# Two gated cross-attention layers over a shared context: keys and values projected by f32 matmuls instead of three f16 ones, and the preparation of a batch laid out anew

## What is computed

```python
x = x + tanh(g_xattn[0]) * L0_xattn(layernorm(x), ctx)         # differential attention
x = x + tanh(g_ffn[0])   * L0_ffn(layernorm(x))                # 8 experts, top 2, and a shared one
x = x + tanh(g_xattn[1]) * L1_xattn(layernorm(x), ctx, mask)   # masked attention, 16 heads of 8
x = x + tanh(g_ffn[1])   * L1_ffn(layernorm(x))

def L0_xattn(q_in, kv):
    q, k, v = q_in @ Wq.T, kv @ Wk.T, kv @ Wv.T                # 32 query/key heads of 4, 16 value heads of 8
    a1, a2 = softmax(q1 k1 / 2) v, softmax(q2 k2 / 2) v
    return rmsnorm(a1 - lam * a2) * subln * (1 - lam_init) @ Wp.T + bp
```

## Time and profile before

| what | value |
|---|---|
| median of 3 runs | 2584.38 us |
| lowest and highest of them | 2583.19 and 3398.32 us |
| the profiled execution, its own time | 2582.84 us |
| its span on the core | 2581.0 us |
| mean granted clock of TensorE | 0.953 |
| first exponential of layer 0 | 140.6 us after the start |
| DMA: read and written in HBM | 141.39 MB and 76.48 MB |

### The profile page before, as it was taken

The page is one execution under the profiler, slowest core; times in us unless marked ns, Lnnn a source line. Parts: engine busy times, 40 slices in busy tenths (PEclk is TensorE's granted clock), DMA queues, the critical chain, the costliest instruction groups (busy, mean ns, idle before and its releaser), DMA issues. The chain is left out here.

```text
span 2581.0 us, 66889 instructions
## 1 busy us (share of the span) xinstructions
PE 2352.3 (91%) x28024; PEld 1277.8 (50%) x28024; DVE 1802.4 (70%) x3165; ACT 1466.8 (57%) x2101; POOL 770.1 (30%) x926
## 2 busy tenths in 40 slices
PE   3699999999999999999995976999999999999798
PEld 2244444444444444444444852555555555555576
DVE  2588888887887888888864554767667767676454
ACT  2156666666666666666673322665566666656422
POOL 4213323333333243233323442121212122221232
PEclk8589999999999999999997986999999999999799
DMA  3533434534534434444401106565566565653100
GB/s 93 109 66 78 96 95 80 101 90 77 110 77 90 105 77 95 98 80 99 97 2 48 32 29 124 109 117 112 114 116 120 110 123 115 127 107 65 50 1 14
DMA packets 152931, 222.40 MB, mean 86 GB/s; under 512 B 45156, under 2 KB 102116, under 8 KB 152132
## 3 DMA queue, kind: packets, MB, share of 16 engines
q1 hardware_dynamic: 152644, 218.29, 40.5%
HBM read 141.39 MB, written 76.48 MB: 84 GB/s over the span
## 5 line engine op out<-in xcount | busy, mean ns | idle before, releaser
L959 ACT ACTIVATE probs<-score_ps 125x896 f32<-125x896 f32 x1152 | 1012.5, 917 | 261.0 <-PE score_ps L863 260.3
L1021 DVE TENSOR_REDUCE max_part<-max_ps 112x1 f32<-112x500 f32 x1538 | 992.2, 670 | 238.9 <-PE max_ps L844 129.3
L879 PE MATMUL acc_ps<-probs,vext 125*32 125x224 f32 (+1 forms) x12288 | 676.4, 315 | 7.1 <-issue 6.2
L1021 DVE TENSOR_REDUCE max_part<-spare_ps 112x1 f32<-112x500 f32 x766 | 513.5, 670 | 118.0 <-PE max_ps L844 105.5
L844 PE MATMUL max_ps<-kstack,qstack 48*112 48x500 f16 x1538 | 518.1, 401 | 25.7 <-DVE max_part L1021 12.9
L879 PEld LDWEIGHTS acc_ps<-probs,vext 125*32 125x32 f32 x12288 | 257.7, 108 | 305.9 <-issue 281.1
L863 PE MATMUL score_ps<-qstack,kstack 50*125 50x224 f16 (+1 forms) x6144 | 386.9, 243 | 1.9 <-ACT probs L959 1.7
L863 PEld LDWEIGHTS score_ps<-qstack,kstack 50*125 50x125 f16 x6144 | 303.6, 134 | 111.4 <-issue 53.4
L844 PE MATMUL spare_ps<-kstack,qstack 48*112 48x500 f16 x766 | 307.0, 401 | 14.9 <-DVE max_part L1021 7.2
L844 PEld LDWEIGHTS max_ps<-kstack,qstack 48*112 48x112 f16 x1538 | 167.0, 128 | 197.6 <-DVE max_part L1021 132.3
L740 POOL TENSOR_TENSOR heads_out<-turned,rden 56x64 f32<-56x64 f32 x192 | 55.2, 288 | 695.6 <-DVE rden L1012 685.5
(11 more groups left out here) (185 smaller groups left out, 2537.3 us busy)
## 6 DMA issues: line engine op xcount, KB each, us to landing
kstack<-k_parts SPq DMA_DIRECT2D x384, 187.5 KB, 6.5
k_parts<-khl SPq DMA_DIRECT2D x128, 375.0 KB, 5.5
ctx_in<-in_ctx SPq DMA_DIRECT2D x32, 750.0 KB
context_parts<-ctxT SPq DMA_DIRECT2D x32, 750.0 KB, 4.8
ctxT<-context_parts SPq DMA_DIRECT2D x32, 750.0 KB, 6.1
qrows<-q_parts SPq DMA_DIRECT2D x384, 7.0 KB, 7.4
qstack<-max_rows SPq DMA_DIRECT2D x384, 0.9 KB
mask_in<-in_mask SPq DMA_DIRECT2D x64, 82.0 KB
```

What stands on the lines that cost most here:

```text
L879: last = nc.tensor.matmul(acc_ps[32 * j:32 * j + 32, TT * S * i:TT * S * (i + 1)].rearrange("p (s c) -> p s c", s=S), vext[n % SLOTS][:, t ...
L959: nc.scalar.activation(probs[t % 2][:, 896 * h:896 * h + 896].rearrange("k (b c) -> k b c", b=2), score_ps[(t * H + h) % 2][0:KT, :, 0:448 ...
L1021: nc.vector.reduce_max(max_part[0:PIECE, u, third:third + 1], room(user)[0:PIECE, 0:TK], AX.X).then_inc(s_red, 1)
```

## The change

- The turned context stays in f32. `ctxT` (two f16 halves), `ctx_in` and `w_parts` go; one buffer `ctx_f` with two slots takes their place. In layer 0 slot 1 is the loaded context and slot 0 the turned one; in layer 1 the two slots hold the contexts of alternate batches, each with its semaphore. The DRAM copy `context_parts` is f32, the same bytes.
- K is one f32 matmul of 500 columns, V is four f32 matmuls of 128 columns. The weights are the f32 ones; the key weight of layer 0 is copied in another order of columns (`wk_order`). Value weights are no longer multiplied by 64.
- T has no low half: ScalarE's copy is all.
- In layer 1 ScalarE copies the keys with their bias to `key_f`, and GpSimd splits them (`split_keys`), as in layer 0.
- The table `where` places the users anew, one a step on side 1, and M on side 0 as before.
- In layer 1 the load of context `n+4` is issued where that of `n+3` stood, and waits for the values of batch `n+2`.

```diff
-        ctx_in = sb("ctx_in", [KT, NKT, D])
-        ctxT = sb("ctxT", [128, 2, SK], F16)
-        w_parts = sb("w_parts", [128, 2, 2, 2, D], F16)
+        ctx_f = sb("ctx_f", [128, 2, NKT * D])
+        wk_order = sb("wk_order", [128, D])
...
-                    for w in range(2):
...
-                        link(nc.vector.tensor_scalar(weight, weight, QK_UP, None, ALU.mult))
...
-                        link(nc.vector.tensor_copy(high, weight))
-                        link(nc.vector.tensor_tensor(low, weight, high, ALU.subtract))
+                    link(nc.vector.tensor_scalar(small[f"WkT{i}"][:, :], small[f"WkT{i}"][:, :], QK_UP, None, ALU.mult))
+                link(nc.vector.tensor_copy(wk_order[:, :].rearrange("p (r h x) -> p r h x", r=2, h=2), halves_first(small["WkT0"][:, :])))
...
     if L is L0:
-        where = {("V", 0): (0, 1), ("F", 0): (1, 0), ("V", 1): (1, 1), ("F", 1): (2, 0), ("V", 2): (2, 1),
-                 ("T", 0): (3, 1), ("K", 0): (4, 1), ("T", 1): (5, 1), ("K", 1): (6, 1), ("M", 0): (7, 0), ("T", 2): (7, 1),
-                 ("K", 2): (8, 1), ("A", 0): (9, 1)}
+        where = {("V", 0): (0, 1), ("F", 0): (1, 1), ("F", 1): (2, 1), ("V", 1): (3, 1), ("T", 0): (4, 1), ("V", 2): (5, 1),
+                 ("K", 0): (6, 1), ("M", 0): (7, 0), ("T", 1): (7, 1), ("K", 1): (8, 1), ("T", 2): (9, 1), ("K", 2): (10, 1),
+                 ("A", 0): (11, 1)}
     else:
-        where = {("V", 0): (0, 1), ("F", 0): (1, 0), ("V", 1): (1, 1), ("F", 1): (2, 0), ("V", 2): (2, 1),
-                 ("M", 0): (7, 0), ("K", 0): (7, 1), ("K", 1): (8, 1), ("K", 2): (9, 1), ("A", 0): (10, 1)}
+        where = {("V", 0): (0, 1), ("F", 0): (1, 1), ("V", 1): (2, 1), ("F", 1): (3, 1), ("V", 2): (4, 1), ("K", 0): (5, 1),
+                 ("K", 1): (6, 1), ("M", 0): (7, 0), ("K", 2): (8, 1), ("A", 0): (10, 1)}
...
                 if L.masked:
-                    sp.wait_ge(s_v, NTHIRD * n)
+                    at_least(sp, s_v, NTHIRD * (n - 1))
...
                     if L.masked:
-                        next_context(n + 3)
+                        next_context(n + 4)
...
-                if L is L0 and n + 3 < B:
+                if n + 3 < B:
                     split_keys(n + 3)
...
-                    for k, (w, x) in enumerate(((0, 0), (1, 0), (0, 1))):
-                        last = nc.tensor.matmul(spare_ps[:, 0:TK], Wk[w], ctxT[:, x, TK * i:TK * i + TK], start=k == 0, stop=k == 2)
+                    nc.tensor.matmul(spare_ps[:, 0:TK], Wk[:, :], ctxT[n % len(ctxT)][:, TK * i:TK * i + TK],
+                                     start=True, stop=True).then_inc(s_ready, 1)
...
-                        for k, (x, w) in enumerate(((0, 0), (0, 1), (1, 0))):
-                            last = nc.tensor.matmul(spare_ps[0:KT, D * t:D * t + D], ctxT[:, x, c:c + KT], Wv[w],
-                                                    start=k == 0, stop=k == 2)
+                        last = nc.tensor.matmul(spare_ps[0:KT, D * t:D * t + D], ctxT[n % len(ctxT)][:, c:c + KT], Wv[:, :],
+                                                start=True, stop=True)
...
-                    nc.scalar.activation(ctxT[:, 0, TK * i:TK * i + TK], spare_ps[:, 0:TK], ACT.Copy).then_inc(s_ctxT, 1)
+                    nc.scalar.activation(ctxT[0][:, TK * i:TK * i + TK], spare_ps[:, 0:TK], ACT.Copy).then_inc(s_ctxT, 1)
...
+                    at_least(act, s_kl, NTHIRD * (n - 1) + i + 1)
+                    key = key_f[:, TK * i:TK * i + TK]
+                    if L.masked:
+                        nc.scalar.activation(key, spare_ps[:, 0:TK], ACT.Identity, bias=small["bk1"][:, :]).then_inc(s_kf, 1)
...
-                    nc.vector.tensor_tensor(ctxT[:, 1, k], spare_ps[:, 0:TK], ctxT[:, 0, k], ALU.subtract).then_inc(s_cl, 1)
...
-                    nc.vector.scalar_tensor_tensor(khl[:, 1, TK * i:TK * i + TK], spare_ps[:, 0:TK], small["bk1"][:, :],
-                                                   khl[:, 0, TK * i:TK * i + TK], ALU.add, ALU.subtract).then_inc(s_kl, 1)
```

More of the change, by code:

```diff
@@ L478, in attend @@
     qstack = [T["qstack"][i][:, 0:PAIRS * GC].rearrange("p (c q) -> p c q", c=PAIRS) for i in range(SLOTS)]
-    Wk, Wv = ([T["w_parts"][:, layer, w, part, :] for part in range(2)] for w in range(2))
+    Wk, Wv = (small["WkT1"] if L.masked else T["wk_order"]), small[f"WvT{layer}"]
     S = L.heads // VH
@@ L984, in drain @@
                 kind, n, i = user
-                if kind in "VAF" or (kind == "K" and L is L0):
+                if kind != "M":
                     return
```

83 lines of the change are left out of this document (29 added, 54 removed).

## The result

| what | before | after |
|---|---|---|
| median | 2585.3 us | 2607.85 us (2607.45 to 2610.76, 4 runs) |
| ratio | 1 | 1.0092, 95% interval [1.0073, 1.0112] |
| span of the profiled execution | 2581.0 us | 2606.4 us |
| first exponential of layer 0 | 140.6 us | 135.4 us |
| a batch of layer 0 between output copies | 39.34 us | 39.24 us |

The forecast was 2412 us in a range of 2390 to 2470. It was wrong, in sign too. By the 2% that the prediction allows for, the measured time counts as no change; the interval lies above 1 all the same. One of the four runs before stood alone at 3398.32 us, and the ratio leaves it out.

A forecast was written before the change was run, and what follows sets the result against it. It took a TensorE - VectorE - TensorE chain to bound layer 0 and TensorE layer 1. Savings of 94 + 65 (batches), 9 + 2 (prologues) and 2 (setup) made 172 off 2582.8; with 1.5 for the median, 2412 us, range 2390 to 2470.

The forecast's parts named there:

- the price of an f32 product: TensorE, both layers: 0.11 us per 128-column f32 matmul; four for values 0.55, one of 500 columns for keys 0.53.
- the keys' far bound: Key projection, both layers: 0.95 us for the 500-column f32 matmul if an f32 column cost as much as four f16 ones.
- Values and keys: TensorE projections, both layers: f32 instead of f16 matmuls save 0.87 us a batch on values and 0.60 on keys.
- The low half on VectorE: Layer 0: dropping VectorE's context subtraction frees the first reduction, 0.55 us for each of three, 1.65 a batch.
- the three-bank reading of layer 0: Layer 0: a TensorE - VectorE - TensorE chain sets the step; the fourth piece waits until the first is reduced; 2.44 us.
- F to side 1, spreading: Layer 0: moving F off the spot between the pairs saves 0.04 us each, 0.1 a batch; spreading itself worth little.
- Layer 1's keys to GpSimd: Layer 1: three 0.74 us subtractions leave VectorE, saving 0.34 of waits and 0.4 of backlog a batch; search hides GpSimd's work.
- Two buffers: Layer 1's context loads: no gain in steady state and none expected in the prologue, between 0 and 5 us.
- The prologues and the setup: Before the layers: 9 us from layer 0's prologue, 2 from layer 1's, 2.4 from fewer weight operations in setup.
- (a): Rival, values and keys: f32 columns cost four f16 ones, values 0.98, keys 0.95, total 2565 us; chance 0.05.
- (b): Rival, layer 1: batch stays 25.1 us through later context load and queued maxima rows, 2477 us; chance 0.12, whole or part.
- (c): Rival, layer 0: key rows arrive late for search at step 7, slower than before, e.g. 2615 us; chance 0.03.

The follow-up runs named there:

- e7: The kernel after, with each key product taking 250 of its 500 columns from the fourth batch on: 2538.5 us.
- e2: The kernel before with f16 products, the turned context's low half left out (zero) and layer 1's keys split by GpSimd: 2534.7 us.
- e1: The kernel after with the kernel before's table of places in both layers: 2615.5 us.
- e6: e5 with the old places in layer 1, keeping two context buffers and the later load: 2536.8 us.
- e9: e6 with layer 1's context load, query rows and mask all issued behind the maxima's rows: 2596.7 us.
- e13: e6 with layer 1's query rows, key fills and context loads left out after the first batches (mask load stays): 2504.1 us.
- e5: e4 with VectorE making the first three batches' low halves, and two context buffers and the new places in layer 1: 2529.0 us.
- e12: e6 with layer 1's query rows loaded behind the maxima's rows: 2534.8 us.
- e11: e5 with layer 1's query rows loaded behind the maxima's rows: 2520.7 us, ratio 0.9725.
- e4: The kernel before with f16 products, ScalarE copying the turned context as f32 and GpSimd splitting it and all keys; nothing left out: 2548.2 us.

## Why the prediction was wrong

**The step that failed** is the price of an f32 product. The prediction put it so: "four f32 matmuls of 128 columns take 0.55 until the next instruction, and in the feed-forward stage 32 in a row take 3.66 us, 0.11 each". Both rows were misread.

- The four of the earlier trace rows (L819) turn a block; they are transposes, recorded once each. A transpose takes about half the time of a product: four of 125 columns are 0.58 above, four products of 128 columns 1.07.
- The 32 of the earlier trace rows are sixteen products: by the code an expert's down projection has four token tiles of two products, eight an expert. So one is 3.66 / 16 = 0.23 us.
- A count would have shown it. In the earlier trace rows the weighing of half a step is four products in the code and x8 in the row.

"Both rows give the same rate" was taken for a confirmation; two wrong readings agreed, since each of the two records of a product is about as long as the one record of a transpose. Against it stood the Trainium skill, "FP8 and Floating Point Precision", section "TensorE Precision Notes", four passes for true FP32. The trace agrees with it: 1.68 ns a column in e7, and 0.23 us for 128 columns in the earlier trace rows, where four passes at 2.4 GHz make 0.213 (an estimate). I had given it one chance in twenty. The prediction did write down 0.95 as the keys' far bound, but left it out of the range, where it would have been 3 x 0.42 x 58 = 73 us.

**Values and keys.** Forecast -0.87 and -0.60 a batch, measured +0.69 and +0.90. That is 3.06 us a batch off in each layer; over the 29 batches of each that still prepare another, 177 of the 196 us that the forecast missed.

**The low half on VectorE.** 1.65 forecast, 1.62 measured (e2). The number bears out the three-bank reading of layer 0. All of it went into the f32 products: 39.34 - 1.62 + 1.59 - 0.07 = 39.24.

**F to side 1, spreading.** Layer 0: 0.1 forecast, 0.07 measured (e1, which moves all users and not F alone). Layer 1: nothing forecast; it costs 0.41 a batch and saves 16 us of extra in this kernel, 27 in the f16 one. This was not in the prediction, and neither was the DMA load behind it: the earlier trace rows with 6.2 us of waits on "issue" was set down as noise of 10 us, where a cause with up to 46 us stood behind it: TensorE's instructions coming late.

**Layer 1's keys to GpSimd.** 0.74 forecast, 0.78 measured. The cover held, no search waited for a fill. Layer 1 in sum: 25.12 + 1.59 - 0.78 + 0.41 = 26.34.

**Two buffers.** Nothing forecast for the batch, nothing found: the regular batch is 24.34 in e2 with one and in e6 with two. (With f16 products and one buffer TensorE waits 5.2 us in all for the context, in e2 between 1600 and 2340 us; with two, nothing.)

**The prologues and the setup.** Forecast 9 + 2.4 for layer 0, measured 5.2. The kernel before, then the kernel after, TensorE's timeline of the first turning and of the keys of two thirds:

```profile
40.45 0.62 PE L794 MATMUL spare_ps<-wide,ctx_in 125*128 125x125 f32 x4 [2.58 <-PEq L324]
...
92.85 1.41 PE L803 MATMUL score_ps<-ctxT,w_parts 128*128 128x500 f16 x3 [1.55 <-DVE ctxT L992]
```

```profile
38.30 0.62 PE L781 MATMUL spare_ps<-wide,ctx_f 125*128 125x125 f32 x4 [2.57 <-PEq L315]
...
83.63 2.00 PE L789 MATMUL score_ps<-ctx_f,wk_order 128*128 128x500 f32 x2 [0.77 <-ACT ctx_f L917]
...
87.24 2.00 PE L789 MATMUL score_ps<-ctx_f,wk_order 128*128 128x500 f32 x2 [0.77 <-ACT ctx_f L917]
```

The setup gave 2.15 of 2.4. The wait of keys for the turned context fell from 1.55 to 0.77, the 0.78 of the forecast. Yet the key products hold TensorE for 1.80 (83.63 to 85.43) instead of 1.19 (89.06 to 90.25), at a granted clock of 0.50 between 80 and 90 us, and a third now takes 3.61 instead of 3.79 (the earlier trace rows and the row above): 0.18 gained where 1.18 was reckoned. Nine thirds make 1.6, and the two waits for the next context fell from 15.2 to 14.3 us in all. From layer 0's last exponential to layer 1's first 0.6 came of the 2 forecast for layer 1's prologue; the dearer keys are the likely reason, which no run separates.

**The rivals.** (a) was the right cause and had 2565 us. It priced the values at 0.98 and the keys at 0.95 by the rate of f16 columns; measured were 1.07 and 1.04. That is 0.09 x 6 = 0.54 a batch in each layer too little, 31 us over 58 batches, and it knew nothing of the 0.41 in layer 1, another 12: with the two it is 2608. That this meets the measured time so closely is luck: it leaves out the 7 us by which layer 1's extra fell, and some 3 that prologues and end gave less than (a) had. (b) did not come: no batch waits for a context or a maxima row. (c) did not come in the kernel after either (TensorE waits for no DMA between 140 and 1200 us), but e9 shows in layer 1 that the mechanism is real.

## What to carry to other kernels

Before a row prices an operation, divide its count by the number of operations that the code issues there, and ask whether it is a product or a transpose: an f32 product stands as two matmul records, a transpose as one. Three f16 products of high and low halves cost less here than one f32 product, and the gain of the idea lay in taking the splitting off VectorE: with f16 products kept and GpSimd splitting, the kernel runs at 0.9725 [0.9687, 0.9763] of the time before. When TensorE stops in the middle of a run of matmuls with no semaphore to wait for, look at the DMA share of that stretch and at when its instruction packets land, not at the engines.

## What the runs showed of the hardware that was not expected

- An f32 product of 500 columns takes 1.04 us until the next instruction, 250 columns 0.62, four of 128 columns 1.07; f32 transposes of 125 columns take 0.58 for four.
- TensorE stalls for up to 2.9 us inside uninterrupted matmuls while the DMA engines are full (e6), 22.1 us in 740; with most transfers gone there are none (e13). After the stall of 2.84 us the granted clock was 0.81 over 8.8 us.
- These stalls end 1.2 to 1.9 us after a 16 KB instruction packet has landed (all 110 in thirteen traces), and stand at one place of every block of 256 of TensorE's matmuls and weight loads.
- The same transfers and the same engine work went with 36 us or 9 us of irregular time, by where in the batch the preparation lies (e6, e5; 30 and 9 in e12 and e11).
- On GpSimd a cast of 128x500 from f32 to f16 takes 0.60 us and the subtraction 1.07: harmless a batch ahead, 14 us in a prologue where it is the chain (e4).
